# The residual's addition and the low part of each normalised tile moved from VectorE to GpSimd, in the first four FFN images of a two-layer metaformer kernel

## The reference

```
def ffn(x, gate_w, gate_b, w1, b1, w2, b2):
    probs = softmax(einsum('bsd,de->bse', x, gate_w) + gate_b)
    masked = probs where it is one of the two largest, else 0
    masked = masked / (masked.sum(-1) + 1e-9)
    h = gelu(einsum('bsd,edh->ebsh', x, w1) + b1)
    y = einsum('ebsh,ehd->ebsd', h, w2) + b2
    return einsum('bse,ebsd->bsd', masked, y)

t = t + ffn(layernorm_over_channels(t), ...)
```

## Time and profile before

| | us |
|---|---|
| median of 3 runs | 1548.86 |
| profiled execution, whole | 1553.49 |
| its span, first to last instruction | 1551.7 |
| PE busy | 1408.4 (91%) |
| DVE busy | 1135.1 (73%) |
| ACT busy | 725.3 (47%) |
| POOL busy | 517.0 (33%) |

### The profile page before, as it was taken

The page is one execution under the profiler, slowest core; times in us unless marked ns, Lnnn a source line. Parts: engine busy times, 40 slices in busy tenths (PEclk is TensorE's granted clock), DMA queues, the critical chain, the costliest instruction groups (busy, mean ns, idle before and its releaser), DMA issues.

```text
span 1551.7 us, 21475 instructions
## 1 busy us (share of the span) xinstructions
PE 1408.4 (91%) x6700; PEld 1053.1 (68%) x6700; DVE 1135.1 (73%) x2875; ACT 725.3 (47%) x1508; POOL 517.0 (33%) x533
## 2 busy tenths in 40 slices
PE   5879688997899999998789999999999999998998
PEld 4656655664556776665556676778888788877786
DVE  6956988699875444489994555686888786799787
ACT  5633353455433444556443444454545454456454
POOL 5051162111810000120360001463346433465575
PEclk9998799998899999999999999999999999999999
DMA  5632235323524222424144212362324322221121
GB/s 125 138 111 68 50 109 150 107 70 83 143 62 118 74 57 71 132 79 113 49 121 125 59 49 50 95 161 59 91 68 125 94 57 69 75 72 55 56 75 53
DMA packets 169602, 136.53 MB, mean 88 GB/s; under 512 B 115120, under 2 KB 162258, under 8 KB 169394
## 3 DMA queue, kind: packets, MB, share of 16 engines
q1 hardware_dynamic: 164514, 129.91, 30.9%
q0 software_dynamic: 3072, 4.82, 1.2%
q10 hardware_dynamic: 1904, 0.43, 0.1%
HBM read 95.47 MB, written 39.30 MB: 87 GB/s over the span
## 4 chain that ended last, share of the span: by engine, by line
PE 56%; issue 16%; DVE 13%; POOL 8%; ACT 6%; SPq 1%; DMA 0%; ACTq 0%; POOLq 0%; DVEq 0%
PE at_ps L1376 10%; PE y_ps L1231 9%; PE h_ps L1238 6%; PE h_ps L1240 6%; PE h_ps L1239 6%; PE y_ps L1220 4%; POOL pix_mem L1109 3%; PE y_ps L1221 3%; PE y_ps L1222 3%; DVE vq_mem L1581 3%; POOL ln_rstd L1082 3%; PE at_ps L1298 2%; ACT ln_cen L895 2%; PE lb_ps L1193 2%; DVE part L1537 2%
## 5 line engine op out<-in xcount | busy, mean ns | idle before, releaser
L1037 ACT ACTIVATE hidden<-h_ps,b 128x448 f32<-128x448 f32 x609 | 384.1, 633 | 609.9 <-PE h_ps L1240 596.2
L1238 PE MATMUL h_ps<-xh,w1h 96*128 96x448 f32 x672 | 366.4, 545 | 5.1 <-ACT pix_mem L940 2.6
L1082 POOL TENSOR_TENSOR ln_rstd<-ln_ve,minus_half 112x4 f32<-112x4 f32 x112 | 166.4, 1486 | 610.0 <-DVE ln_ve L1520 595.5
L1231 PE MATMUL y_ps<-hidden,w 128*96 128x448 f32 x672 | 323.0, 566 | 19.6 <-ACT hidden L1037 13.2
L1537 DVE SCALAR_TENSOR_TENSOR part<-y_ps,b,gate_t 96x448 f32<-96x448 f32 x224 | 151.4, 676 | 203.1 <-PE y_ps L1231 155.3
L1101 POOL CAST in_w<-hidden 128x448 fp32r<-128x448 f32 x273 | 200.2, 737 | 244.4 <-ACT hidden L1037 162.4
L1239 PE MATMUL h_ps<-xl,w1h 96*128 96x448 f32 x672 | 249.8, 372 | 0.0
L1240 PE MATMUL h_ps<-xh,w1l 96*128 96x448 f32 x672 | 249.0, 370 | 0.0
L1238 PEld LDWEIGHTS h_ps<-xh,w1h 96*128 96x128 f32 x672 | 129.8, 193 | 91.9 <-issue 59.5
L1239 PEld LDWEIGHTS h_ps<-xl,w1h 96*128 96x128 f32 x672 | 131.6, 196 | 66.7 <-issue 61.3
L1581 DVE SCALAR_TENSOR_TENSOR vq_mem<-x_mem,all_w,vq_mem 128x770 f32<-128x770 f32 (+1 forms) x168 | 163.7, 1016 | 1.9 <-POOL ln_rstd L1082 0.7
(11 more groups left out here) (186 smaller groups left out, 2123.6 us busy)
## 6 DMA issues: line engine op xcount, KB each, us to landing
gate_t<-gates_dram SPq DMA_DIRECT2D x112, 336.0 KB, 3.3
value_pairs<-pix_mem SPq DMA_DIRECT2D x56, 168.0 KB, 3.2
x_mem<-norm_c SPq DMA_DIRECT2D x16, 420.0 KB, 4.5
x_mem<-norm_a SPq DMA_DIRECT2D x14, 336.0 KB, 4.0
res<-x_attn SPq DMA_DIRECT2D x28, 168.0 KB, 3.0
x_ffn<-ffn_out SPq DMA_DIRECT2D x28, 168.0 KB, 2.0
ln_x<-x_ffn SPq DMA_DIRECT2D x28, 168.0 KB, 3.1
norm_c<-ln_cm SPq DMA_DIRECT2D x28, 168.0 KB, 3.6
```

Of the source, the lines that this page charges most:

```text
L1037: act.activation(to[:, :], h_ps[c % H_BANKS][:, 0:TILE], ACT.Gelu, bias=b1[l][:, c:c + 1]).then_inc(gelu_done, 1)
L1082: pool.tensor_tensor(ln_rstd[n % 2][:, :], ln_ve[n % 2][:, :], minus_half[0:SUB, 0:NSUB], ALU.pow)\
L1231: pe.matmul(y_ps[e % Y_BANKS][0:C, 0:TILE], w2[l][:, c, :], hidden[c % HID_RING][:, :], start=(j == 0), stop=(j == CPE - 1)).then_inc(hid_ ...
L1238: pe.matmul(ps, hi, xh[:, ring(k)], start=True, stop=False)
```

## The change

For slots 0 to 3 `sum_residual` runs on GpSimd, and for every FFN tile that is normalised before slot 4 (35 tiles) `split_tile` does. GpSimd's list gets `pool_residual` of the step before, behind the power of this step's first normalisation job; the split of the late job behind that; and the split of the first job at the end of the step, behind the gathers. The residual of the last tile of slot 3 stands at the end of its own step. `sum_experts` writes into `pair` instead of `part` in all slots; so `combine` of expert 0 waits for `sum_pairs` of the tile before, and `sum_pairs` for the residual of the tile before. SP's list is unchanged.

```diff
+            def pool_residual(u, m):
+                k = TILES * u + m
+                pool.wait_ge(summed, 3 * k + 2)
+                pool.wait_ge(res_ld, 16 * (k + 1))
+                if m > 0:
+                    pool.wait_ge(ffn_st[u], 16 * m)
+                elif u > 0:
+                    pool.wait_ge(ffn_st[u - 1], 16 * TILES)
+                pool.tensor_tensor(ffn_out[:, :], pair[0:C, 0, :], res[:, :], ALU.add).then_inc(summed, 1)
+
+            def pool_split(job):
+                pool.wait_ge(ln_moved, job.n + 1)
+                cols = ring(f_count(job))
+                pool.tensor_tensor(xl[:, cols], ln_cm[job.n % 2][:, :], xh[:, cols].bitcast(F32), ALU.subtract)\
+                    .then_inc(split, 1)
...
                 if 0 in jobs:
                     scale_rows(jobs[0])
+                if slot >= 0 and (slot, p) != (0, 0):
+                    pool_residual(*divmod(TILES * slot + p - 1, TILES))
+                for job in LATE[slot, p]:
+                    if job.kind == "f":
+                        pool_split(job)
                 if 3 in stages and stages[3] == 0:
                     gather(0, 4, 8)
...
                     gather(stages[4], 8 if stages[4] in ON_PE else 12, 2 * GQ)
+                if 0 in jobs and jobs[0].kind == "f":
+                    pool_split(jobs[0])
+                if (slot, p) == (SPLIT_SLOTS[0] - 1, TILES - 1):
+                    pool_residual(slot, p)
...
             def split_tile(job):
+                if job.step[0] < SPLIT_SLOTS[0]:
+                    return
...
-                if e == 0:
-                    dve.wait_ge(summed, 3 * k)
+                if e == 0 and k > 0:
+                    dve.wait_ge(summed, 3 * k - 2)
...
             def sum_pairs(u, m):
...
+                dve.wait_ge(summed, 3 * k)
...
-                dve.tensor_tensor(part[:, 0, :], pair[0:C, 0, :], pair[0:C, 1, :], ALU.add).then_inc(summed, 1)
+                dve.tensor_tensor(pair[0:C, 0, :], pair[0:C, 0, :], pair[0:C, 1, :], ALU.add).then_inc(summed, 1)
 
             def sum_residual(u, m):
+                if u < SPLIT_SLOTS[0]:
+                    return
...
-                dve.tensor_tensor(ffn_out[:, :], part[:, 0, :], res[:, :], ALU.add).then_inc(summed, 1)
+                dve.tensor_tensor(ffn_out[:, :], pair[0:C, 0, :], res[:, :], ALU.add).then_inc(summed, 1)
```

## The result

The changed kernel takes 1571.96 us (median of 4 runs, 1567.43 to 1573.61), the kernel before 1549.16 on the same chip (1548.81 to 1550.23): a ratio of 1.0141, interval 1.0119 to 1.0163, so 22.8 us slower. The prediction said slower, by 5.2 us, and its range ended at 1563.0. The direction and the place were right, the size was not.

A forecast was written before the change was run, and what follows sets the result against it. TensorE was taken to bind most of slots 0 to 3, VectorE where the attention's taps run. Terms -1.5 + 3.2 + 2.7 + 0.8 = +5.2 on the profiled 1553.49 gave 1558.7 us, range 1545.5 to 1563.

The forecast's parts named there:

- slot 1 to 2: Start of (2, 0): late residual delays gates and first combine, TensorE waits 3.3 us instead of 0.61; +2.7, bounds +2.0 and +3.8.
- Slot 0 to 1: Start of (1, 0): residual 6.3 us later holds store and gates; TensorE goes on 3.2 us later, gain included.
- the lead: Before slot 0: four splits off VectorE between 144 and 180 us, less meetings, save 1.5 us; bounds 0 and 2.5.
- the gain: (0, 4) to the indices, likewise (2, 4) to (2, 6): seven instructions off VectorE save 2.7 us, bounds 0 and 4.3.
- Slot 2 to 3: Start of (3, 0): path ends at GpSimd's last power, TensorE at 803 to 804.5; +0.8, gain included, bounds -2.7 and +4.5.
- GpSimd's price: Each of the 63 two-input GpSimd instructions of 448 columns takes 0.93 us, from products of 256 and 896 columns.
- Port: Rival: GpSimd's two-SBUF-input instructions and VectorE's hold each other off, so no gain; +12.7, 1561.6 us; chance 0.19.
- Relief: Rival: VectorE's savings come in full, late gates absorbed if (0, 6)'s residual ends by 398.2; -9.1, 1539.8 us; chance 0.16.
- Cancelled: Rival: gains of some 4 us against +2.7 in (2, 0) and about 1 elsewhere; 1548.9 us; chance 0.15.
- theory 3: From the experiments, not the prediction: GpSimd's longer list, in which gathers and powers come late, makes the loss.

The follow-up runs named there:

- residuals alone: Changed kernel with only the 28 residuals on GpSimd, splits on VectorE as before; 1570.75 us, 1.0131 of the kernel before.
- three residuals: Of the 63 moved instructions only the residuals of (0, 6), (1, 6) and (2, 6) stay on GpSimd; 1565.89 us, 1.0118 of the kernel before.
- gates first: Changed kernel, but SP issues the next slot's first gates ahead of the last tile's store; 1551.88 us, 1.0009 of the kernel before.
- last residual on VectorE: Changed kernel, but the residual of the last tile of slots 0 to 2 back on VectorE; 1549.24 us, 0.9994 of the kernel before.
- splits alone: Changed kernel with only the 35 splits on GpSimd, all residuals on VectorE as before; 1555.16 us, 1.0022 of the kernel before.
- lead on VectorE: Changed kernel with SP's gates ahead of the store and image 0's seven splits back on VectorE; 1550.89 us, 1.0003 of the kernel before.
- before with the gates first: Kernel before, only SP's order changed: next slot's first gates ahead of the last tile's store; 1549.43 us, ratio 0.9996.
- sum alone: Kernel before with only the experts' sum in its own place, all residuals and splits on VectorE; 1549.43 us, ratio 1.0011.
- lead's splits alone: Only image 0's seven splits on GpSimd, the sum in its own place as in the changed kernel; 1551.39 us, 1.0020 of the kernel before.
- quiet steps: Of the 63 moved, 40 stay on GpSimd: slots 0 to 3, residuals of tiles 2 to 5, splits of tiles 0 to 5; 1545.78 us, 0.9974.
- tap slots: Of the 63 moved, 20 stay on GpSimd: residuals of tiles 2 to 5, splits of tiles 0 to 5, slots 0 and 2 only; 1543.22 us, 0.9967.

## Why the prediction was right in its direction and wrong in its size

**Right: the place and the mechanism.** The order on GpSimd, the store behind the residual, the gates behind the store, and the combine that waits by "issue" came as described; the idle times forecast were 10, 11 and 9 us and are 11.21, 11.64 and 10.71. The two experiments with three instructions show it from both sides, 0.9994 without them and 1.0118 with them alone. For slot 1 to 2, where nothing but this chain counts, TensorE's wait was forecast at 3.3 us and is 3.42.

**Wrong: the step Slot 0 to 1.** The forecast put SP's store at 401.4; it came at 406.27, 4.9 us later. 2.8 of these were lost ahead of (0, 5): the lead and (0, 0) to (0, 4) became longer, where the forecast had a gain in the lead. 1.7 are gain that didn't come: (0, 5) and (0, 6) became 1.0 us shorter, not 2.7. And split and residual took 1.14 and 1.12 us instead of 0.93: 0.4. Counted from the start of (0, 5), as the term is, TensorE goes on behind the combine in (1, 2) 5.9 us later than before, not 3.2 (447.99 against 439.32, with (0, 5) beginning at 329.6 and 326.8), and from there to (1, 3) it needs another 1.1. The term was +3.2 with the gain and is 8.0 - 1.0 = +7.0. The bound of +6, set for the case that the gain doesn't come, was the better number.

**Wrong: the path of Slot 2 to 3.** Here the forecast let TensorE run up to GpSimd's last power and priced only what follows from that: +0.8. In the changed kernel TensorE already stands still in (3, 0), 3.45 us for what follows from the first power, which now has gathers and a split ahead of it, and 5.03 us for the first combine. So (3, 0) alone takes 31.6 us instead of 24.1, and of the wait of 4.02 behind the last power at most 2.2 are left. The term is 6.9 - 1.4 = +5.5, beyond its bound of +4.5. This is the largest miss of the sum, 4.7 us.

**Wrong by omission: the clock.** No term of the sum had it. Slot 1 to 2 was forecast at +2.7; the wait grew by 2.8, but the step by 4.5, because behind the longer wait TensorE executes at the lower level for a while, 29.49 us of work instead of 27.80. The upper bound of +3.8 left no room for it. The three profiled kernels with late gates (changed, residuals alone, three residuals) spend 29.4 to 30.4 us of TensorE's time in (2, 0), the other eleven 27.6 to 27.9, so these 1.7 us are shown. The 1.5 and 1.3 of the table in (1, 0) to (1, 2) and (3, 0) to (3, 2) are not: there the eleven scatter from 74.6 to 79.2 and from 73.4 to 77.0. The earlier trace rows had the warning in it: steps with waits stand there at 0.84 to 0.94, the step without at 1.00.

**Wrong: the lead.** Forecast -1.5, bounds -2.5 and 0; it is +1.4 in the profiled execution, and seven splits alone make the kernel 0.05 to 0.34% slower. I took meetings with taps for accidents at 0.35 us apiece, from one row. In the lead they are no accident, and one costs 0.9. TensorE's waiting (length minus busy time) is 47.2 to 49.4 us in the lead of the five profiled kernels with these splits on GpSimd and 46.0 to 47.3 in the other nine: 1.5 us more on average. So the lead loses about what it was to gain, as far as single executions tell. That its full +1.4, and the +1.4 behind it, come from this isn't shown, since TensorE's busy time in the lead scatters from 147.4 to 151.7: the kernel before with only SP's order changed starts slot 0 1.9 us later in its profiled execution, with no instruction of the lead changed.

**Right in number, half in kind: the gain.** Forecast 2.7 at each of slots 0 and 2, 5.4 together; the twenty instructions there alone give 0.33%, 5.1 us. But the waits shrink by only 1.4 us a slot, all of it in (0, 5) and (2, 5), with nothing clear in (0, 6) and (2, 6). The rest is a clock that the forecast didn't have, so that the numbers meet is in part luck. In the changed kernel 2.4 of the 5.4 are seen.

**GpSimd's price.** Taken 0.93 us, measured 1.12 to 1.14 where VectorE is quiet. Eight of the 28 residuals, beside taps, take 2.6 to 5.6. These are the groups over the program, residual and split, and one of the slow ones:

```profile
L1111 POOL TENSOR_TENSOR ffn_out<-pair,res 96x448 f32<-96x448 f32 x28 | 53.7, 1917 | 27.4 <-DVE pair L1576 27.4
L1116 POOL TENSOR_TENSOR xl<-ln_cm,xh 96x448 fp32r<-96x448 f32 x35 | 40.7, 1162 | 21.2 <-ACT ln_cm L915 21.1
```
```profile
239.50 4.34 POOL L1111 TENSOR_TENSOR ffn_out<-pair,res 96x448 f32<-96x448 f32 x1
```

The nearest row by shape, a product of 256 or 896 columns, gave a price 18% too low; that makes 0.2 us each time it stands ahead of SP's store, twice at a slot change with gathers. The Trainium skill's factor (GPSIMD Engine Reference, section 3.1) gave 1.2 us as an estimate, nearer than mine. The Trainium skill's rule on the shared port (SBUF — State Buffer, "SBUF: two separate sides"), that the loser of a meeting blocks fully, agrees within 0.2 us with the tap of 1.89 us: the split ends 1.08 us after the tap's start, and 0.81 are left for the tap, which alone takes some 1.0.

**The rivals.** *Port* was nearest in size, 1561.6, and fell as the main cause: 60 of the 63 instructions stay on GpSimd at 0.9994. The meetings that it describes are there, and the lead pays for them. *Relief* fell; its condition, the residual's end by 398.2, was missed by 8 us. *Cancelled* has the number of the run without the three residuals, but not its mechanism: nothing is lost in (2, 0) there.

**What stays open.** With the gates first the change still doesn't gain its 5 us. TensorE's waiting points at a place. In four profiled kernels a split stands between the gathers and the power, and the gates aren't late (gates first, last residual on VectorE, splits alone, lead on VectorE): TensorE waits 10.7 to 13.3 us in (1, 0) to (1, 2) and 10.9 to 11.7 in (3, 0) to (3, 2). In the six that have neither split nor residual there (before, before with the gates first, sum alone, lead's splits alone, quiet steps, tap slots) it waits 6.6 to 9.8 and 6.8 to 9.6. So GpSimd's longer list, theory 3 in small, seems to cost some 3 us at each of the two places, about what the change gains. No run took that split away alone, so this is argued and not shown. Nor do the parts add up fully: 1.0118 for the three and 0.9994 for the rest make 1.0112 against 1.0141, 4.5 us apart, of which the later gates may explain some 2.7; the intervals cover the rest.

## What to carry to other kernels

Before moving an instruction to another engine, follow its result into the queue that consumes it: a store that waits at the head of an in-order queue holds every load behind it, needed or not, and here three such instructions of 63 cost more than all the rest could bring. Move work off an engine only in the stretches where it binds: twenty instructions gained 0.33%, forty 0.26% (no difference that can be told), sixty-three lost 1.4%. And price a new wait of TensorE with the matmuls behind it, not only with its length.

## What the runs showed of the hardware

- Behind 3.08 us of idle TensorE's products took 1.70 us instead of 0.92. Over all profiles the product behind the tap's wait in (0, 5) and (2, 5) was at the lower level behind 14 of 16 waits of 2.6 to 3.1 us, and behind none of 12 waits of 1.7. In (2, 0) a wait that grew from 0.61 to 3.42 us cost 4.5: 2.8 of waiting and 1.7 of slower matmuls.
- A GpSimd addition of 96x448 takes 1.12 us where VectorE is quiet, 4.34 in a place where it streams taps, and a tap that begins beside one 1.89 instead of some 1.0. The cost falls on both sides.
- Profiled executions of kernels that don't differ in a stretch can differ there by 4 us through the granted clock alone: (2, 5) takes 33.2 us at 0.85 with the sum in its own place, 30.5 at 0.94 before and 28.8 at 1.00 with three residuals alone, and TensorE waits 5.5 to 5.6 us in each.
